# The second attention of a four-layer kernel: scores twice, P formed transposed, masked q and k by DMA

## What is computed

```
x = x + tanh(g_xattn[0]) * L0_xattn(layernorm(x), ctx, ctx)
x = x + tanh(g_ffn[0])   * L0_ffn(layernorm(x))            # experts, one per token
x = x + tanh(g_xattn[1]) * L1_xattn(layernorm(x), ctx, ctx)
x = x + tanh(g_ffn[1])   * L1_ffn(layernorm(x))            # quantised two-layer net
x = x + tanh(g_xattn[2]) * L2_xattn(layernorm(x), ctx, ctx, mask)
x = x + tanh(g_ffn[2])   * L2_ffn(layernorm(x))            # experts, two per token
x = x + tanh(g_xattn[3]) * L3_xattn(layernorm(x), ctx)
x = x + tanh(g_ffn[3])   * L3_ffn(layernorm(x))            # experts, one per token
```

```
qh, kh, vh = split_heads(q @ wq.T + bq), split_heads(k @ wk.T + bk), split_heads(v @ wv.T + bv)
score = einsum('bhqd,bhkd->bhqk', qh, kh) / sqrt(8)
out   = einsum('bhqk,bhkd->bhqd', softmax(score), vh)
return merge_heads(out) @ wo.T + bo
```

## Time and profile before

| | us |
|---|---|
| median of 3 runs | 3624.97 |
| lowest and highest | 3622.75, 3628.83 |
| the profiled execution, its own time | 3616.34 |
| its span (first to last instruction) | 3614.6 |
| stage of the second attention, first DMA issue to the last update of x | 968.65 to 1423.30 |

### The profile page before, as it was taken

How to read it: one execution, slowest core, us unless ns; L and a number is a source line. 1 busy time by engine, 2 the same in 40 slices (tenths; PEclk the granted TensorE clock), 3 DMA queues, 4 the chain that set the end, 5 groups by cost and what they waited for, 6 DMA issues and landing times. The chain is left out here.

```text
span 3614.6 us, 84054 instructions
## 1 busy us (share of the span) xinstructions
PE 2554.5 (71%) x30961; PEld 1981.4 (55%) x30971; DVE 2132.0 (59%) x4394; ACT 1498.5 (41%) x2492; POOL 1596.1 (44%) x2184
## 2 busy tenths in 40 slices
PE   5999999977678886233687766609956877665490
PEld 4878778764557775122465555506634665554260
DVE  3767777661166664676578788854424666677312
ACT  3555555532255553677343333202215665553120
POOL 1333433440164430775024666440017788884207
PEclk9999999988888887555688778659976766675795
DMA  4000000003300000000000000015531000000243
GB/s 143 17 18 22 23 21 21 20 8 112 99 26 22 22 19 13 1 1 1 26 10 12 23 22 23 20 61 153 161 106 32 23 25 27 27 23 13 79 128 93
DMA packets 192979, 153.50 MB, mean 42 GB/s; under 512 B 24426, under 2 KB 170461, under 8 KB 192582
## 3 DMA queue, kind: packets, MB, share of 16 engines
q1 hardware_dynamic: 176198, 116.45, 11.0%
q0 software_dynamic: 16384, 31.69, 2.9%
HBM read 97.54 MB, written 52.43 MB: 41 GB/s over the span
## 5 line engine op out<-in xcount | busy, mean ns | idle before, releaser
L979 PE MATMUL l_B<-l_val,l_prob_t 128*64 128x18 f32 x6144 | 348.6, 220 | 44.1 <-ACT l_prob_t L822 36.9
L979 PEld LDWEIGHTS l_B<-l_val,l_prob_t 128*64 128x64 f32 x6144 | 340.4, 149 | 59.3 <-issue 59.3
L903 PE MATMUL l_PT<-const_table,l_prob 128*128 128x128 f32 x1536 | 267.9, 332 | 38.0 <-ACT l_prob_t L822 28.6
L1971 PE MATMUL experts_H<-experts_xs_t,experts_w 128*128 128x512 f32 x576 | 272.1, 616 | 10.1 <-ACT experts_hid L1951 4.9
L903 PEld LDWEIGHTS l_PT<-const_table,l_prob 128*128 128x128 f32 x1536 | 237.3, 178 | 68.8 <-issue 58.0
L822 ACT COPY l_prob_t<-l_PT 128x512 f32<-128x512 f32 x384 | 209.6, 601 | 132.8 <-PE l_PT L903 132.7
L203 POOL DMA_INDIRECT l_got<-rows,l_index x192 | 220.2, 1147 | 94.7 <-POOL l_index L196 50.3
L358 POOL TENSOR_TENSOR l_products<-l_router_w,xn_all 128x1024 f32<-128x1024 f32 x100 | 236.3, 2390 | 32.3 <-DVE logits L464 32.0
L883 PE MATMUL l_A<-const_table,l_xn 128*128 128x128 f32 x192 | 59.6, 410 | 251.7 <-issue 139.1
L328 POOL DMA_INDIRECT slots<-xn_all,put x192 | 202.0, 1052 | 60.6 <-issue 49.5
L632 POOL TENSOR_TENSOR l_var_eps<-l_mv,eps 128x2 f32<-128x2 f32 x96 | 26.4, 275 | 430.4 <-DVE l_mv L775 430.3
(11 more groups left out here) (309 smaller groups left out, 6835.8 us busy)
## 6 DMA issues: line engine op xcount, KB each, us to landing
experts_w<-in_F_w SPq DMA_DIRECT2D x104, 256.0 KB, 2.9
experts_xs<-slots SPq DMA_DIRECT2D x72, 256.0 KB, 2.8
rows<-experts_y SPq DMA_DIRECT2D x72, 256.0 KB, 2.9
l_ctx_t<-in_ctx_t SPq DMA_DIRECT2D x96, 128.0 KB, 2.1
slots<-l_zeros SPq DMA_DIRECT2D x64, 96.0 KB
experts_w<-in_F_w SPq DMA_DIRECT2D x40, 128.0 KB, 2.5
slots<-l_zeros SPq DMA_DIRECT2D x8, 512.0 KB, 5.5
l_ctx_t<-in_ctx_t SPq DMA_DIRECT2D x64, 64.0 KB, 2.0
```

The lines of the kernel that those rows point to most:

```text
L903: last = nc.tensor.transpose(PT[:, c % 2, P * a:P * a + P], prob[:, t.par(5), c, a // 2, 2 * (a % 2):2 * (a % 2) + 2, :].rearrange("p j k ...
L979: last = nc.tensor.matmul(B[64 * b:64 * b + 64, col:col + 18], prob_t[:, 4 * (hp // 2) + 2 * tile + hp % 2, 64 * b:64 * b + 64], val[:, t. ...
L1971: nc.tensor.matmul(H[:, c, :], w1_s[:, t.par(2), c, :], xs_t[:, t.par(2), :], start=True, stop=True).then_inc(h_filled[c], 1)
```

## The change

Layer 1 calls the new function `attention_split`; `attention_narrow` stays for layers 2 and 3. In the new function:

- The scores are computed twice. S, as before with queries on the partitions, goes into four PSUM banks X and serves the row maximum alone. The maxima (128 rows by 32) are split into three bfloat16 parts, turned by one bfloat16 matmul (L1710 of the changed kernel) and spread by VectorE over `top_d`, with a mask for each of eight columns.
- P is computed with keys on the partitions into four banks Z: first 16 bfloat16 matmuls with a stationary operand of minus ones bring in minus the maximum (L1611), then 16 float32 matmuls of k (stationary) and masked q (moving) add the scores (L1619). ScalarE writes the exponential of it to `prob_t`, in four pieces. Nothing is transposed.
- The masked copies `k_m` and `q_m` have their zeros written once. SyncE fills the blocks with DMAs from SBUF to SBUF, eight partitions of 256 floats each: 16 for k and 16 for q in every beat. ScalarE writes k and q once each.
- P times V has 64 matmuls of 64 rows by 64 columns with 9 moving columns each.
- The biases of values and output come in as bfloat16 rows, prepared once by seven small steps in a row on VectorE. The pipeline is one stage deeper. The masked copies, q and k have three slots, ctx has six.

`Head` gathers with the index columns where they lie, without the copies (layers 1 and 3; in the new function it runs after `combine`). `Router` of the first attention writes `g.xn` from VectorE, and POOL's copy of it (L1111) is gone.

```diff
-        for k in range(self.ks):
-            last = nc.gpsimd.tensor_copy(self.index[:, t.par(s), k, :], g.get[k][:, bass.ds(t.item(s) * 2, 2)])
-        last.then_inc(self.index_done, 1)
+        g = self.g
         for k in range(self.ks):
             for tile in range(2):
+                col = t.item(s) * 2 + tile
                 pool.wait_ge(ready, count)
-                wait(pool, self.index_done, n0)
-                wait(pool, self.terms_done, n2)
+                wait(pool, self.terms_done, t.done(s + 2))
                 pool.indirect_dma_start(self.got[:, t.par(s), k, tile, :], None, self.rows,
-                                        bass.IndirectOffsetOnAxis(ap=self.index[:, t.par(s), k, tile:tile + 1], axis=0),
+                                        bass.IndirectOffsetOnAxis(ap=g.get[k][:, col:col + 1], axis=0),
                                         bounds_check=self.rows.shape[0] - 1, oob_is_err=False).then_inc(self.arrived[t.par(s)], 16)
     def combine(self, nc, pool, t, s, ready, count):
-        g, n1, n2 = self.g, t.done(s), t.done(s + 1)
...
-            pool.wait_ge(self.w_in, self.loads)
-            wait(pool, self.xn_done, n2)
-            nc.gpsimd.tensor_copy(g.xn[:, bass.ds(t.item(s + 2) * k, k), :], self.xn_s[:, t.par(s + 2), :, :]).then_inc(self.xn_kept, 1)
...
+def attention_split(nc, g, name, gate_col, wq, bq, wk, bk, wv, bv, wo, bo, kind, mask=None, head=None, router=None):
...
+    STAT, NORM, TURN, PROJ, SCORE, PROB, OUT, STREAM = range(1, 9)
...
+        q_m = ph.sb("q_m", [P, 3, 4, 256])
+        k_m = None if stable else ph.sb("k_m", [P, 3, 4, 256])
+        val = ph.sb("val", [P, 2, 2, 16, 9])
...
+        X, Z = ph.ps("X", [P, 4, 512]), ph.ps("Z", [P, 4, 512])
+        QK = X[:, 0, :] if stable else Z[:, 0, :]
+        XV = Z[:, 1, :]
+        TOP, WO, TURNED, RANKS = X[:, 0, 0:P], X[:, 1, 0:256], X[:, 2, :], X[:, 3, :]
...
+            sp.wait_ge(cleared, 3)
...
+                if t.live(2):
+                    wait(sp, xv_filled, beats(t.t - 2, TURN, XV_BEATS) if t.t >= 8 else 0)
+                    sp.dma_start(ctx_t[:, t.par(2, 6), :], g.ctx_t[:, t.item(2) * 256:t.item(2) * 256 + 256]).then_inc(ctx_in[t.par(2, 6)], 16)
+                if t.live(PROJ):
+                    slot = t.par(PROJ, 3)
...
+                        wait(sp, qk_drained, t.done(PROJ))
+                        wait(sp, s_filled, t.done(PROJ + 3))
+                        for row in range(0, P, 8):
+                            sp.dma_start(k_m[row:row + 8, slot, row // 8 % 4, :], k_t[row:row + 8, slot, :]).then_inc(k_masked[slot], 16)
+                    wait(sp, qk_drained, t.done(PROJ))
+                    wait(sp, p_filled, t.done(PROJ + 3))
+                    for row in range(0, P, 8):
+                        sp.dma_start(q_m[row:row + 8, slot, row // 8 % 4, :], q_t[row:row + 8, slot, :]).then_inc(q_masked[slot], 16)
+            for t in range(2, ITEMS + PROJ):
+                step(Step(sp, ITEMS, t))
...
+                    wait(dve, s_filled, n5)
+                    V.tensor_reduce(top[:, :, :].rearrange("p r a -> p (r a)"), X[:, :, :].rearrange("p r (a k) -> p (r a) k", k=64),
+                                    AX.X, ALU.max).then_inc(top_done, 1)
+                    dve.wait_ge(ready, 1)
+                    wait(dve, top_done, n5)
+                    wait(dve, top_filled, t.done(SCORE + 1))
+                    V.tensor_copy(split[:, :, 0, :], top[:, :, :]).then_inc(hi_done, 1)
...
+                    V.tensor_tensor(split[:, :, 2, :], rest[:, :, :], split[:, :, 1, :], ALU.subtract).then_inc(split_done, 1)
...
+                    dve.wait_ge(ready, 1)
+                    wait(dve, top_filled, n5)
+                    wait(dve, p_filled, t.done(SCORE + 2))
+                    V.tensor_tensor(top_d[:, t.par(SCORE), :, :], TOP.unsqueeze(1).broadcast_to([P, 8, P]),
+                                    g.const[:, C_AMASK:C_AMASK + 8].unsqueeze(2).broadcast_to([P, 8, P]), ALU.mult).then_inc(diag_done, 1)
...
+                        wait(act, o_filled, t.done(PROB + 2))
...
+                            nc.scalar.activation(prob_t[:, t.par(PROB), r, :], Z[:, r, :], ACT.Exp).then_inc(prob_done, 1)
...
+                    nc.scalar.activation(k_t[:, t.par(PROJ, 3), :], QK[:, 256:512], ACT.Identity, bias=bk_s[:, :])
+                    nc.scalar.activation(q_t[:, t.par(PROJ, 3), :], QK[:, 0:256], ACT.Identity, bias=bq_scaled[:, :],
+                                         scale=SCALE).then_inc(qk_drained, 1)
...
+                    wait(pe, q_masked[slot], 16 * reused(t, PROB, 3))
...
+                        wait(pe, diag_done, n6)
...
+                        for tile in range(2):
+                            for b in range(2):
+                                for r in range(4):
+                                    rows = slice(32 * r, 32 * r + 32)
+                                    nc.tensor.matmul(Z[64 * b:64 * b + 64, r, 256 * tile:256 * tile + 256], minus_ones[rows, :],
+                                                     top_d[rows, t.par(PROB), 4 * tile:4 * tile + 4, 64 * b:64 * b + 64],
+                                                     start=tile == 0, stop=False)
+                    for tile in range(2):
+                        for b in range(2):
+                            for r in range(4):
+                                rows = slice(32 * r, 32 * r + 32)
+                                seq = slice(128 * tile + 64 * b, 128 * tile + 64 * b + 64)
+                                last = nc.tensor.matmul(Z[64 * b:64 * b + 64, r, 256 * tile:256 * tile + 256], k_t[rows, slot, seq],
+                                                        q_m[rows, slot, :, seq], start=stable and tile == 0, stop=tile == 1 and not folded)
...
+                    wait(pe, k_masked[slot], 16 * reused(t, SCORE, 3))
...
+                                last = nc.tensor.matmul(X[64 * b:64 * b + 64, r, 256 * tile:256 * tile + 256], q_t[rows, slot, seq],
+                                                        k_m[rows, slot, :, seq], start=not folded and tile == 0, stop=tile == 1)
+                    last.then_inc(s_filled, 1)
...
+                    terms = (prob_t, soft) if stable else (prob_t,)
+                    for h in range(16):
+                        for tile in range(2):
+                            for b in range(2):
+                                rows, side = slice(64 * b, 64 * b + 64), 64 * (b ^ tile)
+                                for k, term in enumerate(terms):
+                                    col = 256 * tile + 64 * (h % 4)
+                                    last = nc.tensor.matmul(Z[side:side + 64, 2 + b, 9 * h:9 * h + 9], term[rows, t.par(OUT), h // 4, col:col + 64],
+                                                            val[rows, t.par(OUT), tile, h, :],
+                                                            start=k == 0, stop=k == len(terms) - 1)
...
+                    wait(pe, split_done, n5)
+                    nc.tensor.matmul(TOP, split[:, :, :, :].rearrange("p r s a -> p (r s a)"), g.const_bf[:, C_IDENT:C_IDENT + P],
+                                     start=True, stop=True).then_inc(top_filled, 1)
...
         attention_wide(nc, g, t, (t["F0_wg"], t["F0_bg"], "first", first_rows))
         rows0 = moe(0, first_rows, "first", "gelu", 4)
-        attention_narrow(nc, g, "l1", 1, t["L1_wq"], t["L1_bq"], t["L1_wk"], t["L1_bk"], t["L1_wv"], t["L1_bv"],
+        attention_split(nc, g, "l1", 1, t["L1_wq"], t["L1_bq"], t["L1_wk"], t["L1_bk"], t["L1_wv"], t["L1_bv"],
                          t["L1_wo"], t["L1_bo"], "softmax", head=(rows0, 1, True))
...
```

More of the change, by code:

```diff
@@ L52, in constants @@
     c[:, C_BLK:C_BLK + 16] = np.arange(16) * SLOTS
-    c[:, C_ITEM:] = np.arange(TOP2_TILES)
+    c[:, C_ITEM:C_AMASK] = np.arange(TOP2_TILES)
+    for a in range(8):
+        c[:, C_AMASK + a] = np.arange(P) % 8 == a
     return c
@@ L183, in __init__ @@
         self.g, self.rows, self.ks, self.own = g, rows, ks, own
-        self.index = ph.sb("index", [P, 2, ks, 2], U32)
         self.got = ph.sb("got", [P, 2, ks, 2, D])
-        self.term = ph.sb("term", [P, ks + own, 2, D])
+        self.term = ph.sb("term", [P, 2, 2, D])
         self.arrived = [ph.sem(f"arrived{k}") for k in range(2)]
-        self.index_done, self.terms_done, self.combined = ph.sems("index_done terms_done combined")
-        self.partly = [ph.sem(f"partly{k}") for k in range(ks + own - 1)]
+        self.terms_done, self.partly, self.combined = ph.sems("terms_done partly combined")
@@ L210, in combine @@
-        landed = t.landed(s, 2 * self.ks)
-        tiles = bass.ds(t.item(s) * 2, 2)
+        g, par, n = self.g, t.par(s), t.done(s)
+        tiles = slice(t.item(s) * 2, t.item(s) * 2 + 2)
         xs = g.x[:, tiles, :]
+        others = (self.got[:, par, 0, :, :], g.xn[:, tiles, :] if self.own else self.got[:, par, 1, :, :])
         pool.wait_ge(ready, count)
```

(28 more changed lines are left out.)

447 lines of the change are left out of this document (407 added, 40 removed).

## The result

The changed kernel takes 3886.77 us (median of 4 runs, 3879.35 to 3903.32) against 3626.9 us of the kernel before in the same comparison (4 runs, 3622.75 to 3630.59). The ratio is 1.072, 95% interval 1.069 to 1.076: slower by about 260 us. The forecast was 3714 us, 3635 to 3805. The sign and the bound that it named are right; the size is not, and the time lies above the range.

The account below looks back on a forecast made before the run. SyncE's DMA issues were taken to bound the changed second attention at 16.0 us a beat. 3616.3 + 117 (second attention) - 27.5 (Head, fourth attention) = 3705.8, plus 8.6 up to the median: about 3714 us, range 3635 to 3805.

Parts of the forecast that it names:

- The sign: Whole kernel: the change makes it slower, chance 0.88; faster 0.09, same 0.03.
- SyncE is the bound: Second attention: SyncE issues 33 DMAs a beat without rest and PE follows it; 16.0 us a beat.
- The price of an issue: SyncE, second attention: one DMA issue takes 0.475 us whatever its size, so 33 take 15.7 us a beat.
- the formula of the prediction: Whole kernel's time from the second attention's beat b: 3714 + 32 x (b - 16.0) us.
- b: The second attention's time for one of its 32 beats, forecast as 16.0 us.
- Dearer issues: Rival, SyncE's queue: 0.57 us an issue gives 3804 us, 0.86 us gives 4111 us; chance 0.12, half over 3804.
- Setup and ends: Second attention: first k DMA at 1014, 32 SyncE beats to 1526, 14 us behind; stage ends at 1540, +117 us.
- the rival of slow P times V: PE, second attention: P times V as slow per instruction as before, 7.5 us instead of 2.3; 3762 us, chance 0.05.
- The sum of 10.1 us at full clock: PE's beat, second attention: 11.97 - 5.81 + 1.12 + 0.5 + 2.3 = 10.1 us, below SyncE's.
- Head in the fourth attention: POOL: gathers without index copies save 0.86 us of its 19.93 us beat, -27.5 us over 32 beats.
- VectorE takes over as the bound: Rival, fourth attention: the gathers gain nothing, 27 us more than forecast, 3741 us; no separate chance given.
- the break-even: SyncE, second attention: the time equals that of before at b = 13.2 us, an issue of 0.40 us.

Follow-up runs that it names:

- masks-on-ScalarE kernel: Changed kernel without the 32 masked DMAs a beat; ScalarE writes q_m and k_m from PSUM in eight passes: 3510.37 us, ratio 0.971 to the kernel before.
- the full runs: Changed kernel with the old attention_narrow for the second attention, leaving only the Head and Router changes: 3588.0 us against 3619.11 of the kernel before, ratio 0.9915.
- the two pairs of profiles: Kernel before and kernel with only Head and Router changed, each profiled twice: fourth attention 708.0 and 708.3 us before, 693.4 and 690.8 us with the new Head.

## Why the prediction was wrong in size, point by point

**SyncE is the bound: right.** No gap in its queue, PE idle before L1652, the clock down (0.57, a little lower than the 0.6 to 0.75 that were said), and with the masked DMAs gone the stage falls to a beat of 10.41 us. That the q and ctx issues hide every wait of SyncE was right too.

**The price of an issue: the step that failed.** I took 0.475 us from the earlier trace rows, "the value that didn't depend on size", with 0.57 and 0.86 as upper bounds. So the term 33 x 0.475 = 15.7 us a beat was mis-sized: measured were 0.625 us, 0.67 from start to start, and 33 x 0.67 = 22.1 us. That this lay below the upper bound of 0.86 us was luck, since no row bounded this kind of DMA. The independence of size was true of it, and the runs confirm that from 8 to 128 rows. But all rows read DRAM and write SBUF, and the trace of before had none from SBUF to SBUF (from SBUF to DRAM it had 0.434 us, `slots` from l_zeros, which gives no warning either); what I varied was size and shape, not where source and destination lie. That kind of DMA costs twice one of its own shape from DRAM. In the formula of the prediction, b = 22.23 instead of 16.0 adds 32 x 6.23 = 199 us, which is more than the whole error of 173 us.

**The chances.** "Dearer issues" had 0.12, and only half of that above the range. The dearest row was 0.86 us. For a kind of DMA that no row showed, the range should have reached at least to that (28.4 us a beat, 4111 us), or that side should have had more than the 6% which were left outside.

**Setup and ends: 23 us too much at the front.** I had the first projection 12 us later than the 1000.49 us of the earlier trace rows and the first k DMA at 1014. It was issued at 991.3, and the projection for q ran at 989.2, 11 us earlier than before (3 us of this lie ahead of the stage, which begins at 965.6 instead of 968.7). The fills (2.66 us on GpSimd) and the chain of small steps cost 2.6 of the 5 us: the first gather stands 9.9 us behind the stage's first DMA (975.57) instead of 7.3. The 7 us for one more stage in the pipeline did not appear at the start at all. GpSimd's first reciprocal deviation step stands at 985.0 instead of 990.8, with one pair of gathers ahead of the first `combine` where there were two; that is 6 of the 11 us. The rest stands behind it: the first projection follows the first `xn` after 3.0 us instead of 8.5. At the end I allowed 14 us behind the last q, and from the last q issue to the last update of x there are 20, at half clock. Together about -17 us.

**TensorE: right where it counted, and generous.** P times V was said to take 2.3 us at full clock and not 7.5; in the masks-on-ScalarE kernel 128 of its instructions take 2.21 us. So the earlier trace rows was the right row for the 64x64 tile. The Trainium skill's section "Instruction Overhead", in the page "TensorEngine Tiling (Array Packing)", would have given the rival of slow P times V; the trace doesn't bear that rival out here. The sum of 10.1 us at full clock was too high: PE's busy time is 9.3 us a beat (195.89 of 220 us, at a beat of 10.41), at a clock of 0.83. The sum started from the beat of 11.97 us, of which PE was busy for 10.14, and so took 1.8 us of idle time along.

**The time of initiating DMAs.** 0.625 us of issue beside a landing of about 2 us is small once and, 33 times, the whole beat. The Trainium skill's page "DMA: Bandwidth & Descriptors", section "Issuing engines are not separate DMA queues", calls that time usually small beside the DMA. The trace decides against what the prediction drew from this, that SyncE would not be the bound; for one DMA it has 0.625 us beside about 2. The page's rule to coalesce ("Rules for kernel authors") is worth about 350 us here, though not for the overhead of small transfers with which it argues: what is saved is the issuing engine's time.

**Head in the fourth attention: half of it.** The copies and their wait did go, 0.86 us a beat, and a rival of the prediction (VectorE takes over as the bound) had it half right as well: GpSimd ran into VectorE in some beats, and 12.9 of 27.5 us went back. Late in the stage, where the earlier trace rows was read, its beat of about 20 us mostly fell to between 18.5 and 19.5 us (said: 19.1). But the beats of this stage go from 10 to 22 us, and in the middle some, of 17 to 19 us, gained nothing, so one beat did not stand for 32. What the full runs show of Head and Router together, 24 to 38 us, is more than the 15 to 18 us of that stage; the spans of the two pairs of profiles differ by 23.0 and 16.6 us. Where the rest comes from isn't settled: single profiles of one stage differ by up to 10 us.

**Sum of the profile.** 3714 us, less the 8.6 us between median and profile, plus 199 (issues), minus 17 (ends), plus 15 (Head), is 3902; the profiled execution took 3888. What is behind the second attention and is not the fourth took 18 us less (11 of it in the third attention, whose code did not change and where it may be spread), and the second attention took 4 us more than these terms give. Neither was followed.

## What to carry to other kernels

Count the DMAs that one queue must issue in a beat, and price each by a row of the same kind of source and destination, not only of the same size. A price from another kind is no estimate and not even a sure bound, and the break-even (here 0.40 us an issue) says how much of the range it decides. Where data only has to be masked or moved between partitions that a compute engine can reach in one pass, compare the passes (3.9 us on an engine with room) with the issues (21 us on a queue), and where DMAs must do it, lay the data out so that few do.

## What the runs showed of the hardware

SyncE's issue of a DMA, median: 0.295 us from DRAM to SBUF with 8 rows; 0.37 to 0.46 us from SBUF to DRAM (`out`, `slots`, `rows`); 0.625, 0.589, 0.594 and 0.601 us from SBUF to SBUF with 8, 16, 32 and 128 rows. In the changed kernel the gap behind one is 0.04 us, and the longest issue took 1.67 us; a burst of 16 takes 10.66 us in the median and 10.85 on average. Why from SBUF to SBUF is dear, no run tells.

The same ctx DMA (128 rows from DRAM) had 0.333 us in the kernel before, 0.352 among DRAM DMAs of 8 rows, 0.439 behind SBUF-to-SBUF DMAs of 8 rows, and 0.58 to 0.59 behind those of 16, 32 and 128 rows. So an issue's time also depends on what was issued ahead of it; why was not tried.

With SBUF-to-SBUF issues on ScalarE at the same time, SyncE's took 13% longer (704 ns against 625). ScalarE's took 727 ns in the median and 631 at least.
